# The bias row of two experts, from TensorE products to an addition on POOL

## The reference, cut to what matters

```
x = x + gnn(layernorm(x), src, dst, edge_weight, W, b)        # 200000 edges
xn = layernorm(x)
w, (e0, e1) = gates of the two best experts for mean(xn)
out = sum over k of w[k] * (gelu(xn @ W1[ek] + b1[ek]) @ W2[ek] + b2[ek])
x = x + layernorm(out + xn) * gamma + beta
```

## Time and profile before

| | us |
|---|---|
| median of 3 runs | 2396.34 (2394.18 to 2400.32) |
| profiled execution, its own time | 2394.09 |
| span of the profile, first to last instruction | 2392.3 |
| tail, from about 1980 us to the end | about 412 |
| mean granted TensorE clock | 0.986 |

### The profile page before, as it was taken

One profiled execution on the slowest core, in us unless ns is written; L12 is line 12 of the kernel. 1 busy time (PEld: TensorE's weight loads), 2 busy tenths in 40 slices (PEclk: granted clock), 3 DMA queues, 4 the chain that ended last, 5 costly groups with the idle time before them and its releaser, 6 DMA issues.

```text
span 2392.3 us, 41714 instructions
## 1 busy us (share of the span) xinstructions
PE 2218.0 (93%) x9986; PEld 1736.1 (73%) x9987; DVE 1028.9 (43%) x2973; ACT 1194.0 (50%) x3203; POOL 1596.2 (67%) x1626
## 2 busy tenths in 40 slices
PE   2488998999999999999999999999998999999998
PEld 1366776776776777777777777777776777999998
DVE  7882233232232223233223323232321245898888
ACT  3577667665565555545534433332324116665664
POOL 6777777777777777777777777777777771332231
PEclk9999999999999999999999999999999999999999
DMA  9855667565655655656656665655565543333321
GB/s 372 332 171 159 198 203 250 175 191 181 187 181 178 184 178 170 192 177 186 187 178 189 186 183 178 192 172 174 183 193 173 180 147 121 118 116 106 132 89 54
DMA packets 226740, 425.79 MB, mean 178 GB/s; under 512 B 36675, under 2 KB 134774, under 8 KB 226600
## 3 DMA queue, kind: packets, MB, share of 16 engines
q0 software_dynamic: 75008, 204.90, 28.6%
q1 hardware_dynamic: 151160, 217.12, 27.6%
q10 hardware_dynamic: 432, 2.40, 0.3%
HBM read 341.53 MB, written 82.75 MB: 177 GB/s over the span
## 4 chain that ended last, share of the span: by engine, by line
PE 84%; ACT 6%; DVE 4%; issue 3%; DMA 2%; ACTq 0%; DVEq 0%; POOL 0%; SPq 0%; POOLq 0%
PE ps L1442 25%; PE ps L1425 17%; PE ps L1414 17%; PE ps L1563 8%; PE ps L1393 3%; PE ps L1532 3%; PE ps L1542 3%; PE ps L1535 3%; PE ps L1404 2%; PE ps L1405 1%; DVE OH L1086 1%; PE ps L1389 1%; ACT zv L709 1%; PE ps L1398 1%; ACT L703 1%
## 5 line engine op out<-in xcount | busy, mean ns | idle before, releaser
L587 POOL DMA_INDIRECT G<-xr_d,SRC x1467 | 1391.6, 949 | 446.9 <-issue 299.5
L1086 DVE TENSOR_SCALAR OH<-CST,DL,WR 128x128 f32<-128x128 f32 x1564 | 569.2, 373 | 1270.3 <-PE ps L1442 1135.8
L1442 PE MATMUL ps<-G,OH 128*128 x3128 | 740.0, 389 | 79.7 <-DVE OH L1086 59.5
L1442 PEld LDWEIGHTS ps<-G,OH 128*128 128x128 f32 x3128 | 597.2, 194 | 226.1 <-issue 145.4
L1425 PE MATMUL ps<-W2u,H 128*128 128x256 f32 x1920 | 428.9, 381 | 7.2 <-issue 6.4
L1414 PE MATMUL ps<-YU,W1u 128*128 128x512 f32 (+1 forms) x1024 | 426.4, 569 | 9.6 <-ACT H L782 8.5
L1425 PEld LDWEIGHTS ps<-W2u,H 128*128 128x128 f32 x1920 | 361.5, 190 | 69.3 <-issue 21.2
L1414 PEld LDWEIGHTS ps<-YU,W1u 128*128 128x128 f32 x1024 | 195.1, 191 | 206.2 <-issue 184.8
L790 ACT ACTIVATE YE<-ps 128x512 f32<-128x512 f32 (+1 forms) x128 | 72.6, 569 | 440.7 <-PE ps L1425 440.6
L782 ACT ACTIVATE H<-ps,b1a 128x512 f32<-128x512 f32 (+1 forms) x256 | 168.6, 661 | 226.1 <-PE ps L1414 225.8
L667 ACT ACTIVATE OHX<-OHT,WR 128x128 f32<-128x128 f32 x194 | 67.4, 394 | 211.5 <-PE ps L1442 208.6
(11 more groups left out here) (230 smaller groups left out, 2373.9 us busy)
## 6 DMA issues: line engine op xcount, KB each, us to landing
W1u<-in_W SPq DMA_DIRECT2D x64, 512.0 KB
W2u<-in_W SPq DMA_DIRECT2D x64, 512.0 KB
y_d<-YE SPq DMA_DIRECT2D x56, 512.0 KB
G<-xr_d,SRC POOLq DMA_INDIRECT x1467
x_d<-X SPq DMA_DIRECT2D x98, 128.0 KB
yt_d<-YT SPq DMA_DIRECT2D x98, 128.0 KB, 3.3
XR<-in_x SPq DMA_DIRECT2D x97, 128.0 KB, 3.2
XL<-x_d SPq DMA_DIRECT2D x24, 512.0 KB, 4.6
```

Of the source, the lines that this page charges most:

```text
L587: e.indirect_dma_start(out=G[0:rows(s), held(s), :], out_offset=None, in_=x if s < FRESH else xr_d, in_offset=bass.IndirectOffsetOnAxis(ap ...
L1086: e.tensor_scalar(OH[:, s % OHR, :], iota, DL[:, s:s + 1], WR[:, s + 1:s + 2], ALU.is_equal, ALU.mult).then_inc(s_oh, 1)
L1442: e.matmul(ps[:, 0, 0:D], OH[:, r, :], Gf[:, bass.ds(g + r * D, D)], start=False, stop=True, skip_group_check=True).then_inc(s_main, 1)
```

## The change

The bias products L1568, L1596 and L1601 are dropped, and the last product of each accumulator closes it instead. `bias_rows` stops after `B2`. POOL adds `B2` to `XN` in all 25 groups, and DVE's `total` and `finish` wait for POOL's `s_xb` in every group. The tiles `B2h`, `B2l`, `B2t`, `B2r` go, so that the tiles laid out behind them lie 5 KB lower in each partition.

```diff
@@ layout
-        B2h, B2l, B2t, B2r = late("B2h", [P, D], f32r), late("B2l", [P, D], f32r), late("B2t", [P, D]), late("B2r", [P, 2, D], f32r)
@@ POOL, add_rows(n)
                 e.wait_ge(s_xn, n + 1)
-                if g < AHEAD:
-                    e.wait_ge(s_b2, 2)
-                    e.tensor_tensor(out=XN[:, n % 3, 0:m, :], in0=XN[:, n % 3, 0:m, :], in1=B2[:, :].unsqueeze(1).to_broadcast([P, m, D]), op=ALU.add).then_inc(s_xb, 1)
+                e.wait_ge(s_b2, 2)
+                e.tensor_tensor(out=XN[:, n % 3, 0:m, :], in0=XN[:, n % 3, 0:m, :], in1=B2[:, :].unsqueeze(1).to_broadcast([P, m, D]), op=ALU.add).then_inc(s_xb, 1)
                 e.wait_ge(gb_in, 32)
                 e.tensor_tensor(out=XL[:, n % 4, 0:m, :], in0=XL[:, n % 4, 0:m, :], in1=be_bc[:, :].unsqueeze(1).to_broadcast([P, m, D]), op=ALU.add).then_inc(s_xp, 1)
@@ DVE, bias_rows()
                 e.scalar_tensor_tensor(out=B2[:, :], in0=b2s[:, 1, :], scalar=r1[:, 14:15], in1=B2[:, :], op0=ALU.mult, op1=ALU.add).then_inc(s_b2, 1)
-                e.wait_ge(s_b2, 2)
-                e.tensor_copy(B2h[:, :], B2[:, :]).then_inc(s_b2, 1)
-                e.wait_ge(s_b2, 3)
-                e.tensor_tensor(out=B2l[:, :], in0=B2[:, :], in1=B2h[:, :].bitcast(f32), op=ALU.subtract).then_inc(s_b2, 1)
-                e.wait_ge(s_b2, 4)
-                e.tensor_scalar(B2t[:, :], B2l[:, :].bitcast(f32), ident[:, 1:2], None, ALU.mult).then_inc(s_b2, 1)
-                e.wait_ge(s_b2, 5)
-                for c in range(2):
-                    e.scalar_tensor_tensor(out=B2r[:, c, :], in0=B2h[:, :].bitcast(f32), scalar=ident[:, 0:1], in1=B2t[:, :], op0=ALU.mult, op1=ALU.add).then_inc(s_b2, 1)
@@ DVE, total(n, k, some)
-                        if g >= AHEAD:
-                            e.wait_ge(s_xn, n + 1)
-                        else:
-                            e.wait_ge(s_xb, g + 1)
+                        e.wait_ge(s_xb, n + 1)
@@ TensorE, down(k, i)
-                        ins = e.matmul(acc, hp[:, h, rows], wp[:, x_, f, :], start=(i == 0 and q % 2 == 0 and a == 0), stop=False, skip_group_check=True)
-                if i == HID - 1:
-                    e.wait_ge(s_b2, 7)
-                    for q in range(0, m, 2):
-                        w = min(2, m - q) * D
-                        ins = e.matmul(ps[:, 2 * (k % 2) + q // 2, 0:w], ones_r[:, :], B2r[:, :, :].rearrange("p c d -> p (c d)")[:, 0:w], start=False, stop=True, skip_group_check=True)
+                        ins = e.matmul(acc, hp[:, h, rows], wp[:, x_, f, :], start=(i == 0 and q % 2 == 0 and a == 0), stop=(i == HID - 1 and a == 2), skip_group_check=True)
                 ins.then_inc(s_pdn, 1)
@@ TensorE, last group
-                if i == HID - 1:
-                    ins = e.matmul(ps[:, 2 * (k % 2), :], ones_r[:, :], B2r[:, :, :].rearrange("p c d -> p (c d)"), start=False, stop=True, skip_group_check=True)
                 ins.then_inc(s_pdn, 1)
@@
-                    products(acc, k, i, q, i == 0)
-                e.matmul(acc, ones_r[:, :], B2r[:, 0, :], start=False, stop=True, skip_group_check=True).then_inc(s_pdn, 1)
+                    ins = products(acc, k, i, q, i == 0)
+                ins.then_inc(s_pdn, 1)
```

More of the change, by code:

```diff
@@ L1581, in products @@
                 for a, (hp, wp) in enumerate(((Hhi, W2h), (Hhi, W2l), (Hlo, W2h))):
-                    ins = e.matmul(acc, hp[:, h, rows], wp[:, x_, f, :], start=(start and a == 0), stop=False, skip_group_check=True)
+                    ins = e.matmul(acc, hp[:, h, rows], wp[:, x_, f, :], start=(start and a == 0), stop=(i == HID - 1 and a == 2), skip_group_check=True)
                 return ins
```

## The result

The changed kernel takes 2404.95 us in the median of seven runs (2404.19 to 2407.47), the kernel before 2394.51 in seven (2393.84 to 2400.32). The ratio is 1.0041 with a 95% interval of 1.0032 to 1.0051: slower by 10 us. The forecast was 2407 us. The profiled execution took 2407.47 us, its span is 2405.6.

A forecast was written before the change was run, and what follows sets the result against it. TensorE bounds the tail, DVE close behind. With DVE becoming the bound (chance 0.58), `finish` starts 10.9 us later: execution 2394.09 + 10.9 = 2405.0, plus 2.25 to the median, 2407 us; own range 2402 to 2412, overall 2390 to 2413.

The forecast's parts named there:

- bias products, alone: On TensorE in the tail: dropping two products in each of 16 groups saves 0.45 us a group, 7.2 us.
- price of a whole addition, DVE late: In the tail: each POOL addition takes 2.14 to 2.18 us from DVE when DVE always has work.
- pair of groups: Two late-running tail groups on DVE: 33.7 us own work plus six additions at 2.17, 46.7 us, against TensorE's 45.1.
- `Hlo` of (4,4) starts: Beginning of the tail, on DVE: three new additions lie before it, making it 6.5 us later than 2099.55.
- TensorE's stall at `up(5,4)`: Beginning of the tail: TensorE, ready at 2105.9, waits 2.0 us for ACT's instructions behind a late `Hlo`.
- step (6,0) of DVE: In the tail: four new additions ahead of it move it from 2126.93 by 8.7 us to 2135.6.
- two ways to run: Later tail: six additions make 43.3 us a pair where DVE has idle time, 46.7 where late; the tail's beginning decides.
- rival of full gain: In the tail: DVE keeps or regains its idle time and all 7.2 us stay, 2389 us; chance 0.12.
- half-way rival: In the tail: DVE's backlog dissolves at 0.6 us a pair, 2391 to 2396 us, no difference; chance 0.20.
- Late loads of `XL`: In the tail: a late DVE delays these loads, 1 us a pair more, 5 us in all, 2412 us; chance 0.07.
- A new wait on the bias row: On DVE in the tail: it stalls for late POOL additions, one wait being 5 us, about 2401 us; chance 0.03.
- Five instructions fewer in `bias_rows`: On DVE at step (0,7): worth nothing, at most 3.5 us if DVE were late there.

The follow-up runs named there:

- no additions: The changed kernel with POOL's bias addition kept for the early groups alone, so post groups get no bias row: 2388.49 us against 2395.58, 0.9972.
- the version beside `total`: The changed kernel with post-group additions cut in two halves, held back until DVE's next work is `total` and statistics: 2391.91 us against 2398.89, 0.9971.
- the half additions: The changed kernel with POOL adding the bias row to two of four tiles in post groups, the others going without: 2387.42 us, 0.997.
- the version with products and additions both: The kernel before, bias products kept, with POOL's additions and waits of the changed kernel put in: 2407.21 us, 1.0048.
- zeros: The changed kernel with POOL filling its own 8 KB tile with zeros in post groups instead of adding the bias row: 2386.8 us, 0.9966.

## Why the prediction was right

The forecast held in sign, in mechanism and nearly in size: the tail is 10.2 us longer (10.9 forecast), the medians are 10.4 us apart, and 2405 stands for 2407. By its steps, the places of the changed kernel taken 3.0 us earlier for the later start of its tail:

| step | forecast | measured |
|---|---|---|
| bias products, alone | -7.2 us | -6.8 (no additions) |
| price of a whole addition, DVE late | 2.14 to 2.18 us | 2.15: two more make the pair 46.67 us in place of 42.38 |
| pair of groups | 46.7 us | 46.67 |
| `Hlo` of (4,4) starts | 2106.1 (6.5 after 2099.55) | 2105.7 |
| TensorE's stall at `up(5,4)` | 2.0 us | 1.75 |
| TensorE's idle time per pair | 1.6 us | 1.3 to 1.8, and once 4.2 in the last group |
| step (6,0) of DVE | 2135.6 | 2135.2 |
| step (16,0) of DVE | 2369.1 | 2368.9 |
| `finish` starts | 2385.0 | 2384.4 |
| wait of `total` for `s_xb` | nothing | none listed |

**The price.** It was read where DVE had no idle time, so that the whole stretch showed; its mean over the tail would have been less. Some of the 0.7 us by which the sum was too high lies in the last 16 us, where 15.9 were forecast and 15.5 passed.

**The Trainium skill's rule.** The Trainium skill, page SBUF — State Buffer, section "Who interferes with whom", says that a DVE instruction with two SBUF inputs contends with a GpSimd instruction that reads SBUF, and that the second to start is blocked. The runs agree in both directions: L1251 stretched to 2646 ns at most beside an addition, L1230 (PSUM and SBUF) never over 420; and the version beside `total` moves the additions to where there is nothing to block. Only a price of 2.5 us, the whole length of an addition, which the prediction set beside its own, is not borne out: one DVE instruction slips between two additions, and 2.1 to 2.2 are lost.

**The step that failed.** "In the settled part the four additions cost less ... six would make 43.3 us, under 45.1. There are thus two ways to run, and the beginning of the tail decides." The price of 1.6 us was an average over additions of which some fell into idle time, and idle time is used up by the first additional ones. With whole additions from the eighth post group on, DVE's idle time was gone in the same stretch, and its pair 46.68 us. There is one budget, 33.7 us and 2.2 an addition, and it is over TensorE's 45.1 from whatever state it starts; the state is only a lead, lost at 1.6 us a pair. For the change itself that made no difference, since it starts late. It does for the rival of full gain, which leant on the settled part: its threshold, (45.1 - 33.7)/6 = 1.9 us an addition, is what decides, and the half additions lie below it: 44.46 us a pair. They also show the half-way rival's mechanism, a late DVE that catches up at about 0.6 us a pair, below that threshold alone.

**The other rivals.** Late loads of `XL`: one wait of 7.6 us, as before. A new wait on the bias row: none; its 2401 us was also a wrong sum, for with TensorE still the bound the 7.2 us of the products stay gained, 2396.3 - 7.2 + 5 = 2394 us. Five instructions fewer in `bias_rows`: not tried by themselves, but the version with products and additions both keeps them and has the changed kernel's tail to 0.3 us, and the gain without additions is that of the products alone.

**The end of the tail.** The last `Hlo` starts 2372.36 - 2010.85 = 361.5 us after the first `XN` before, and 2366.73 - 2012.02 = 354.7 with no additions in the post groups: 6.8 us earlier. That is 15 x 0.45. The bias products of the sixteenth group come behind the last `up` (at 2372.00 us before), so that nothing ahead of `finish` waits for them: the forecast's term of 7.2 us should have been 6.8. The versions with zeros and with half additions gain a further 1.2 us for another reason. Before, and without additions, POOL's last beta addition begins 1.1 us ahead of the last `Hlo` and stretches it to 1.85 us; behind the zeros it begins after it. Without additions, and with zeros:

```profile
2366.73 1.85 DVE L1217 TENSOR_TENSOR Hlo<-Ht,Hhi 128x512 fp32r<-128x512 f32 x1 [2.42 <-ACT Hhi L909]
```

```profile
2366.37 0.69 DVE L1222 TENSOR_TENSOR Hlo<-Ht,Hhi 128x512 fp32r<-128x512 f32 x1 [2.42 <-ACT Hhi L914]
```

With half additions the last `Hlo` takes 0.74 us.

**Open.** The zeros differ from the addition in more than that they read nothing: another operation, another tile, a shorter time. No run changes the reading alone. That each tail is one profiled execution stays a limit for differences of a few tenths.

## What to carry to other kernels

Before work is moved from the bound engine to an idle one, add up what the idle engine's instructions take from the third: here POOL had room in every stretch, and its additions cost DVE 2.1 to 2.2 us each, which cost the kernel 17 us against 7 gained. Do that sum per period, own work plus price times count against the bound's period, with a price measured where the victim has no idle time: here half additions, under the bound, cost nothing at all, and whole ones, over it, were paid in every pair once DVE's lead was used up. And where a helper has slack in time, choose what it runs beside: held back to DVE's work on PSUM and statistics, the same additions cost nothing, and the change became worth 6.9 us.

## What the runs showed of the hardware

- Four DVE instructions with two SBUF operands take 1.66 us alone and beside POOL's MEMSET of 128x2048 (1.81 us), and 3.8 us beside a POOL TENSOR_TENSOR of 128x1024 (2.4 to 2.6 us).
- POOL pays too: with additions from the eighth post group on, its last bias addition took 4.87 us in place of 2.4, beside DVE's `give` and three `Hlo` (3.3 us in another place of that run); and in the same run a DVE TENSOR_SCALAR of 128x4 took 1.73 us in place of 0.17 beside the beta addition, though it has one tile as its operand. The latter was seen in one place.
- Held back to DVE's PSUM plus SBUF addition and its statistics, the 34 half additions of 128x512 took 1.30 us in the median, and DVE's L1247 never over 424 ns.
